# State-space stage of a decoder kernel: step sizes projected straight into token layout, and another order around it

## What is computed

```
zxbcdt = X @ W_in.T
z, xBC, dt = split(zxbcdt)                 # dt: 16 heads
dt  = softplus(dt + dt_bias)               # step sizes, token x head
xBC = silu(causal_conv4(xBC) + conv_b);  x, B, C = split(xBC)
dA  = exp(dt * -exp(A_log))
h_t = h_(t-1) * dA_t + dt_t * B_t x_t      # state recurrence, per head
y   = (C_t h_t + D * x) * silu(z);  y = rmsnorm(y) * norm_w
out = y @ W_out.T
```

## Time and profile before

| | |
|---|---|
| time, median of 3 runs | 1925.21 us (1923.62 to 1928.34) |
| profiled execution: time, span | 1927.49 us, 1925.8 us |
| busy share: TensorE, VectorE, ScalarE, GpSimd | 95%, 74%, 65%, 24% |
| mean granted clock of TensorE | 0.981 of full |
| state-space stage | about 0 to 810 us; a turn of its loop takes 97.06 us (line 581 starts at 386.26, 483.32 and 580.36) |

### The profile page before, as it was taken

How to read it: one execution, slowest core, us unless ns; L and a number is a source line. 1 busy time by engine, 2 the same in 40 slices (tenths; PEclk the granted TensorE clock), 3 DMA queues, 4 the chain that set the end, 5 groups by cost and what they waited for, 6 DMA issues and landing times. The chain is left out here.

```text
span 1925.8 us, 38879 instructions
## 1 busy us (share of the span) xinstructions
PE 1821.9 (95%) x12684; PEld 1299.9 (68%) x12684; DVE 1433.7 (74%) x2902; ACT 1257.5 (65%) x3128; POOL 469.1 (24%) x661
## 2 busy tenths in 40 slices
PE   7899999999999999778999999999999998799988
PEld 5677777777777778555666666666666664588853
DVE  8988888888888888646686867677777766655348
ACT  5646464646454555348888888888989887356514
POOL 1312121212121212331323232322323233100006
PEclk9999999999999999888999999999999999999999
DMA  7123131313131312333333333434343423811266
GB/s 236 53 55 97 49 103 49 103 47 105 46 105 44 107 45 88 135 100 97 88 111 111 111 111 101 121 90 123 89 121 91 124 70 122 280 48 59 73 205 254
DMA packets 121580, 200.60 MB, mean 104 GB/s; under 512 B 23856, under 2 KB 46384, under 8 KB 121136
## 3 DMA queue, kind: packets, MB, share of 16 engines
q1 hardware_dynamic: 112176, 179.21, 30.3%
q0 software_dynamic: 9216, 18.89, 3.9%
HBM read 117.27 MB, written 29.88 MB: 76 GB/s over the span
## 5 line engine op out<-in xcount | busy, mean ns | idle before, releaser
L2026 DVE TENSOR_REDUCE a_mx<-a_shared 128x1 f32<-128x512 f32 x512 | 329.1, 682 | 51.1 <-PE a_shared L2156 49.7
L1963 ACT ACTIVATE a_shared<-a_shared,a_mx 128x512 f32<-128x512 f32 x512 | 341.0, 668 | 23.4 <-DVE a_mx L2026 23.1
L1956 ACT ACTIVATE a_probs<-a_scores 128x512 f32<-128x512 f32 x512 | 300.7, 600 | 69.7 <-PE a_scores L2173 65.6
L2156 PE MATMUL a_shared<-a_ks,a_qs 96*128 96x512 f32 x512 | 208.9, 428 | 15.2 <-ACT a_shared L1963 10.9
L2173 PE MATMUL a_scores<-a_qs,a_ks 98*128 98x512 f32 x512 | 201.7, 405 | 6.1 <-ACT a_probs L1956 5.9
L2128 PE MATMUL a_shared<-link 128*128 128x512 f32 x768 | 199.4, 396 | 1.1 <-DVE a_qk_lo L2013 1.1
L1083 PE MATMUL m_proj<-m_xt_hi,link 128*128 128x512 f32 x448 | 182.0, 406 | 4.1 <-DVE m_acc L777 3.5
L2156 PEld LDWEIGHTS a_shared<-a_ks,a_qs 96*128 96x128 f32 x512 | 94.3, 190 | 130.7 <-ACT a_shared L1963 59.5
L597 ACT ACTIVATE m_xw<-m_added,m_wdt 128x64 f32<-128x64 f32 x256 | 56.0, 330 | 192.9 <-DVE m_xdt L865 192.8
L1084 PE MATMUL m_proj<-m_xt_lo,link 128*128 128x512 f32 x448 | 176.5, 394 | 0.0
L1085 PE MATMUL m_proj<-m_xt_hi,link 128*128 128x512 f32 x448 | 176.0, 393 | 0.0
(11 more groups left out here) (306 smaller groups left out, 3892.6 us busy)
## 6 DMA issues: line engine op xcount, KB each, us to landing
m_dec<-step_decay SPq DMA_DIRECT2D x64, 256.0 KB, 4.1
a_qs<-link SPq DMA_DIRECT2D x256, 64.0 KB, 2.1
m_ce<-run_decay SPq DMA_DIRECT2D x128, 112.0 KB, 3.0
a_ks<-a_k_hi POOLq DMA_DIRECT2D x192, 64.0 KB, 2.5
e_x<-x SPq DMA_DIRECT2D x11, 1024.0 KB, 5.6
m_xt_in<-x_t_in SPq DMA_DIRECT2D x8, 1024.0 KB, 9.5
m_x_tok<-x_in SPq DMA_DIRECT2D x8, 1024.0 KB, 5.4
x<-m_x_tok SPq DMA_DIRECT2D x32, 256.0 KB, 2.8
```

The costliest lines, as they stand in the source:

```text
L1956: act.activation(probs[:, n % 2, h, :], scores[t.score_bank(n, h)][:, :], ACT.Exp, scale=-1.0).then_inc(exp_ready, 1)
L1963: act.activation(scored[:, :], scored[:, :], ACT.Exp, scale=-1.0, bias=mx[:, i % 2, h, j:j + 1], accum_out=den[:, i, j, h:h + 1]).then_inc ...
L2026: dve.tensor_reduce(mx[:, i % 2, h, j:j + 1], bank(what)[:, :], AX.X, ALU.min).then_inc(mx_ready, 1)
L2156: pe.matmul(bank(what)[:, :], qs[0:STACK, t.slot(i), h, j * P:(j + 1) * P], ks[0:STACK, t.slot(i), h, :], start=True, stop=True).then_inc( ...
```

## The change

`dt_proj` keeps its place but swaps its operands: the 128-token slices of x are stationary and `w_dt` moves, so that the result is in token layout at once (32 matmuls of 32 columns instead of 8 of 512). ScalarE's copy and TensorE's turning matmuls go, and with them `dt_ch` and `pair_sum`; VectorE adds the high and low parts with one more instruction. On VectorE `raw_sizes` comes ahead of `states`, and `softplus` ahead of the B/C convolution. On ScalarE `step_exponents` comes ahead of the B/C tile's first tap. On TensorE x tile 0 comes ahead of `carried_outputs`. `tile_done` counts 17 for a sequence instead of 18, and `DT_STEPS` is 13 instead of 12.

```diff
--- before.py
+++ after.py
@@ -140,7 +140,6 @@
         win_hi, win_lo = (link[:, n * KT * COLS:(n + 1) * KT * COLS].rearrange("p (k c) -> p k c", k=KT)
                           for n in range(2))
         w_dt = sb("w_dt", [P, KT, 2 * NH], F32R)
-        pair_sum = sb("pair_sum", [2 * NH, NH])
         def over(name, tiles):
             return nc.alloc_sbuf_tensor_at("m_" + name, [P, tiles, SEQ], F32R, offset=-(-nc.sbuf_base // 32) * 32)
 
@@ -168,7 +167,6 @@
         xt_hi = sb("xt_hi", [P, KT, SEQ], F32R)
         xt_lo = sb("xt_lo", [P, KT, SEQ], F32R)
         x_tok = sb("x_tok", [P, TT, DM])
-        dt_ch = xt_in[0:2 * NH, 0, :]
         dt = sb("dt", [P, CH, NH])
         a = sb("a", [P, NH, CH])
         decay_t = sb("decay_t", [NH * CH, P])
@@ -216,7 +214,7 @@
         outp = [ps("outp0"), ps("outp1")]
         added = ctx.enter_context(nc.psum_tensor("m_added", [P, 2 * 512], F32))
         misc, turn = added[:, 0:512], added[:, 512:1024]
-        steps = proj[0]
+        steps = proj[0][:, 0:TT * 2 * NH].rearrange("p (c w h) -> p c w h", c=TT, w=2)
         mean = turn[:, 3 * CH * NH + P:3 * CH * NH + P + TT]
         xk_bank = [turn, outp[0]]
         yp = [ps("y0"), ps("y1")]
@@ -239,8 +237,7 @@
         x_in = sem("x_in")
         x_dbl = sem("x_dbl")
         tile_done = sem("tile_done")
-        dt_read = sem("dt_read")
-        dt_turned = sem("dt_turned")
+        dt_done = sem("dt_done")
         a_ready = sem("a_ready")
         sums_done = sem("sums_done")
         wd_ready = sem("wd_ready")
@@ -314,8 +311,9 @@
         next_stage = [(3, 1.0), (1, 1.0), (0, -SOFT_SCALE), (2, 1.0)]
 
         block = ctx.enter_context(nc.Block())
-        SET = 9
-        DT_STEPS = 12
+        SET = 8
+        DT_STEPS = 13
+        TILES = 1 + 2 * XT_TILES
         EARLY = 5
         DEC_CHUNK = 3
         CAST_FROM = 5
@@ -331,7 +329,6 @@
                 if not first:
 
                     sp.wait_ge(xt_split, at(b, KT, 0))
-                    sp.wait_ge(dt_turned, at(b, 1, 0))
                 sp.dma_start(xt_in[:, :, :], one(xT, b).rearrange("a (k p) n -> p (a k) n", p=P)
                              ).then_inc(xt_landed, 16)
 
@@ -419,7 +416,7 @@
                 for gr in range(2, NG):
                     load_carried(b, first, gr)
                 if not more:
-                    sp.wait_ge(tile_done, 18 * n_seq)
+                    sp.wait_ge(tile_done, TILES * n_seq)
                     for n, source in enumerate((one(ctxT, 0).rearrange("a (k p) n -> p (a k) n", p=P),
                                                 *(wT[w].rearrange("(k p) n -> p k n", p=P) for w in (1, 0, 2)))):
                         if n == 1:
@@ -469,8 +466,6 @@
             for r in range(2):
                 ins = pool.memset(parity[r * Q:(r + 1) * Q, r, :], 1.0)
             ins.then_inc(const, 1)
-            pool.tensor_tensor(pair_sum[:, :], ident[0:2 * NH, 0:NH], ident[0:2 * NH, NH:2 * NH], ALU.add
-                               ).then_inc(const, 1)
             pool.wait_ge(const, SET)
             def sum_squares(b, first, gr):
                 for j in range(2):
@@ -532,7 +527,7 @@
         def _(act):
             def conv_tap0(b, n, tile, slot):
 
-                act.wait_ge(tile_done, at(b, 18, tile + 1))
+                act.wait_ge(tile_done, at(b, TILES, tile))
                 act.activation(acc[:, slot, :], proj[tile % 2][:, :], ACT.Identity, bias=cb[:, n:n + 1],
                                scale=cw[:, n, 3:4]).then_inc(taps0, 1)
 
@@ -540,7 +535,7 @@
 
                 if not first:
 
-                    act.wait_ge(tile_done, at(b, 18, 0))
+                    act.wait_ge(tile_done, at(b, TILES, 0))
                 act.wait_ge(xt_landed, at(b, 16, 16))
                 for k in range(KT):
                     act.activation(xt_hi[:, k, :], xt_in[:, k, :], ACT.Copy).then_inc(xt_hi_s, 1)
@@ -571,14 +566,8 @@
 
             def z_silus(b, gr):
                 for j in range(2):
-                    act.wait_ge(tile_done, at(b, 18, 2 + 4 * gr + 2 + j + 1))
+                    act.wait_ge(tile_done, at(b, TILES, 2 + 4 * gr + 2 + j))
                     act.activation(zs[:, gr % 2, j, :], z_bank(gr, j)[:, :], ACT.Silu).then_inc(z_ready, 1)
-
-            def raw_steps(b, first):
-                act.wait_ge(tile_done, at(b, 18, 1))
-                if not first:
-                    act.wait_ge(dt_turned, at(b, 1, 0))
-                act.activation(dt_ch, proj[0][0:2 * NH, :], ACT.Copy).then_inc(dt_read, 1)
 
             def bc_tap0(b, first):
                 if not first:
@@ -609,8 +598,6 @@
             def gate_highs(b, part, more):
                 if part == 0 and more:
                     act.wait_ge(xt_split, at(b, KT, 2 * KT))
-                elif part == 1 and more:
-                    act.wait_ge(dt_turned, at(b, 1, 2))
                 for k in SPLIT_GATES[part]:
                     ins = act.activation(gate_high(k, more), g[:, k, :], ACT.Copy)
                 ins.then_inc(sq_ready, 1)
@@ -634,9 +621,9 @@
                 ins.then_inc(wd_ready, 1)
 
             def step_exponents(b):
-                act.wait_ge(dtv, at(b, DT_STEPS, 3))
+                act.wait_ge(dtv, at(b, DT_STEPS, 4))
                 act.activation(sm[:, 2], sm[:, 1], ACT.Exp).then_inc(dta, 1)
-                act.wait_ge(dtv, at(b, DT_STEPS, 4))
+                act.wait_ge(dtv, at(b, DT_STEPS, 5))
                 act.activation(sm[:, 4], sm[:, 3], ACT.Ln).then_inc(dta, 1)
 
             def bc_silus(b, first):
@@ -653,7 +640,6 @@
                 x_high(b, True)
                 act.wait_ge(small_in, 16 * N_SMALL)
                 act.activation(aneg[:, :], aneg[:, :], ACT.Exp).then_inc(dta, 1)
-                raw_steps(b, True)
                 bc_tap0(b, True)
                 step_exponents(b)
                 x_tap0(b, True, 0)
@@ -682,7 +668,6 @@
                 act.activation(wout_hi[:, :, :], wout_part, ACT.Copy).then_inc(const, 1)
 
             def next_head(done, b):
-                step_exponents(b)
                 x_tap0(b, False, 0)
                 bc_silus(b, False)
                 for j in range(2):
@@ -699,8 +684,6 @@
                         x_high(b + 1, False)
                     weighted_x(b, first, gr)
                     if gr + 1 == NG:
-                        if more:
-                            raw_steps(b + 1, False)
                         act.wait_ge(g_ready, gated_at(b, SPLIT_GATES[0][-1]))
                         gate_highs(b, 0, more)
                     if gr + 1 < NG:
@@ -713,6 +696,7 @@
                     if gr + 1 < NG:
                         silus(b, first, gr + 1)
                     elif more:
+                        step_exponents(b + 1)
                         bc_tap0(b + 1, False)
                     if first and gr == 0:
                         cast_columns(7)
@@ -792,16 +776,17 @@
             def raw_sizes(b, first):
 
                 dt_chain.start(b)
-                dve.wait_ge(dt_turned, at(b, 1, 1))
-                dt_chain.link(dve.tensor_tensor(sc[0].rearrange("p (c h) -> p c h", h=NH),
-                                                steps[:, 0:CH * NH].rearrange("p (c h) -> p c h", h=NH),
-                                                dtb[:, :].unsqueeze(1).to_broadcast([P, CH, NH]), ALU.add))
+                dve.wait_ge(dt_done, at(b, 1, 1))
+                raw = sc[0].rearrange("p (c h) -> p c h", h=NH)
+                dt_chain.link(dve.tensor_tensor(raw, steps[:, :, 0], dtb[:, :].unsqueeze(1).to_broadcast([P, CH, NH]),
+                                                ALU.add))
+                dt_chain.link(dve.tensor_tensor(raw, steps[:, :, 1], raw, ALU.add))
                 dt_chain.link(dve.tensor_scalar(sc[5], sc[0], -1.0, None, ALU.mult))
                 dve.tensor_tensor(sc[1], sc[0], sc[5], ALU.min).then_inc(dtv, 1)
 
             def softplus(b):
 
-                dt_chain.start(b, 3)
+                dt_chain.start(b, 4)
                 dve.wait_ge(dta, at(b, 2, 2))
                 dt_chain.link(dve.tensor_scalar(sc[3], sc[2], 1.0, None, ALU.add))
                 dt_chain.link(dve.tensor_scalar(sc[7], sc[3], 1.0, None, ALU.is_equal))
@@ -811,8 +796,8 @@
 
             def step_sizes(b, first):
 
-                dt_chain.start(b, 7)
-                dve.wait_ge(dtv, at(b, DT_STEPS, 7))
+                dt_chain.start(b, 8)
+                dve.wait_ge(dtv, at(b, DT_STEPS, 8))
                 dve.wait_ge(dta, at(b, 2, 3))
                 dt_chain.link(dve.tensor_tensor(sc[4], sc[4], sc[6], ALU.mult))
                 dt_chain.link(dve.tensor_tensor(sc[5], sc[4], sc[7], ALU.add))
@@ -830,7 +815,7 @@
                 dve.wait_ge(wd_ready, at(b, 2, 1))
                 if not first:
                     dve.wait_ge(decay_out, at(b, 32, 0))
-                dt_chain.start(b, 11)
+                dt_chain.start(b, 12)
                 for r in range(2):
                     half = slice(r * Q, (r + 1) * Q)
```

(32 more changed lines are left out.)

## The result

The kernel after takes 1970.86 us (median of 4 runs, 1965.92 to 1971.84), the kernel before 1924.41 (4 runs, 1921.74 to 1928.34): a ratio of 1.0228, with a 95% interval of 1.020 to 1.0256. So it is slower, as forecast, but by 46 us where the forecast had 18, and outside its range.

What follows compares the result with a forecast made beforehand. The prediction took TensorE's queue to set the pace. Head 3.9, first boundary 4.9, six boundaries at 0.71 and clock falls 5 summed to +18 us, put on the median as 1943 us, range 1929 to 1958.

Steps and rivals of the forecast that it cites:

- One record for each small matmul: Step projection on TensorE: each of 32 matmuls issued once, 0.11 us, 3.55 us together; the two-pass rival had chance 0.08.
- The gap of 81 ns: Step projection: the skill's spacing for load and matmul pairs, by which it would take 2.6 us; not used.
- The waits for `m_xw`: TensorE at the state matmuls: a 0.5 us wait that lies inside the new projection and goes.
- at the second z tile: TensorE later in the turn: a 0.54 us wait that goes, since VectorE has 1.18 us less to do there.
- x tile 0 does not wait for the step sums: TensorE at the boundary: VectorE's reads of the sums fit its idle time of about 1 us, costing nothing.
- The wait at x tile 1: TensorE waits 1.62 us for the B/C convolution, late behind softplus and step exponents; the no-wait rival had chance 0.07.
- A boundary without the clock: Between two sequences: -0.37 + 1.62 - 0.54 = +0.71 us, bounds -0.9 and +4.3.
- The head: Before the loop: the first projection at half clock, 6.7 us instead of 3.4, moving VectorE by +3.9 us.
- the first boundary: First change of sequence: projection and states at half clock, 9.7 us against 5.9; with the waits +4.9 us.
- the clock's term: Other six boundaries: half-clock falls of 0.5 to 2.7 us, 1.6 taken at three, +5; the unchanged-clock rival had chance 0.20.
- B: Start of the B/C tile on TensorE at a boundary, forecast at 485.8, 0.37 us earlier than before.
- the six boundaries +4.3: The boundaries after the first, without the clock: 6 x 0.71 us in the sum.

Runs made afterwards that it cites:

- experiment 6: Kernel after, loop start moved by 64 instructions, with three unused wide matmuls for every eight small ones of the projection: 1960.37 us, ratio 1.0184 to the kernel before.
- experiment 3: Kernel after plus 40 empty instructions ahead of the head, new projection kept but all engines' orders put back as before: 1951.69 us, ratio 1.0142.
- experiment 4: Kernel after plus 40 empty instructions, softplus put back behind the B/C convolution and step exponents behind its first tap: 1952.2 us, ratio 1.0145.
- experiment 5: Kernel before with softplus, step exponents and first x tile moved as in the change, old projection and turning step kept: 1932.7 us, ratio 1.0046.
- experiment 7: Kernel after plus 40 empty instructions, B/C tile's 12 wide matmuls among the small ones, its convolution ahead of states, both x tiles ahead of carried outputs: 1950.55 us.
- e1: Kernel after with 80 already satisfied waits (40 instructions) on TensorE ahead of the head, moving the loop's start: 1949.45 us, ratio 1.0123 to the kernel before.
- e3: The run of experiment 4: kernel after plus 40 empty instructions, softplus and step exponents in their old places: 1952.2 us, ratio 1.0145.
- e4: The run of experiment 3: kernel after plus 40 empty instructions, new projection with every old order: 1951.69 us, ratio 1.0142.
- e5: The run of experiment 7: kernel after plus 40 empty instructions, B/C tile's matmuls among the small ones, B/C convolution and x tiles moved earlier: 1950.55 us, ratio 1.0134.
- e6: The run of experiment 6: kernel after, loop start 64 instructions further on, 12 unused wide matmuls at each projection: 1960.37 us, ratio 1.0184.

## Why the prediction was too low

Right, point by point. One record for each small matmul, 0.11 us at full clock and 0.21 at half: 3.48 us from the first to the start of the last, so 3.6 for all where 3.55 was forecast, and 6.6 in the head where 6.7 was. The gap of 81 ns that the Trainium skill gives ("TensorE: Matmul & The Clock Gate", Back-to-back issue gap) is not that of this type and shape; the row of L1226 was the better guide. The waits for `m_xw` and at the second z tile are gone, and x tile 0 does not wait for the step sums. The wait at x tile 1 was forecast as 1.62 us and is 1.4 where the clock stays full (experiment 6); in the kernel after it is 1.0 at most, since falls ahead of it hide it in part. A boundary without the clock was forecast as +0.71; by experiment 6 it is 20.70 - 16.81 = 3.89, less the added 6.24 - 3.48 = 2.76, so +1.13 up to the decay sums, and -0.74 behind them: +0.39. The head (+3.9 forecast, +4.65 measured) and the first boundary (+4.9 forecast, 5.3 - 0.74 = +4.6 measured) were sized well.

Mis-sized, the clock's term: "what comes ahead of B doubles. That is 0.5 to 2.7 us, and I take 1.6 at three of the six: +5". The clock falls at six of six, and costs (19.6 - 6 x 1.13) / 6 = 2.1 us each, +12.8. The forecast took its falls as a matter of chance, from rows in which 128-column work with pauses was at the half level; the traces show that the new projection brings a fall at each boundary, with TensorE busy throughout (experiments 3 and 4, with little or no wait at x tile 1; and in the kernel after every fall begins 1.3 to 4.4 us behind the projection's start, ahead of that wait), that this wait and the new orders bring none (experiments 5 and 6), and that wide matmuls in between mostly prevent it (experiments 6 and 7). Why such matmuls lower the clock no run shows.

Left out, and the largest: no term for the jump of the loop. The sum went through the boundary's engines and never asked what else the 64 more instructions on TensorE do. They move the loop's start to a place where only two transposes get done behind the jump before TensorE stops: +18.9 us, about as much as the whole forecast. With head +3.9, first boundary +4.9, the six boundaries +4.3 and the clock +5 the forecast has 18; measured are 4.65, 4.6, 2.3 and 12.8, and 18.9 for the jumps: 43. Without the jumps the change would have been at e1's 1949 us, inside the range of 1929 to 1958, but with a clock term two and a half times the forecast's: the total alone would have hidden that.

That moving the start moves, shortens and removes the stop is shown (five positions, counted from the kernel before: 0 no stop, 48 1.9 us, 64 2.8 us, or 2.6 in the kernel after, 104 in e1, e3, e4 and e5 none, 128 in e6 none). That the stop is a wait for instructions on their way is argued, from "issue" and from the 1.2 to 1.5 us between the packet's end and the next matmul in all fifteen stops; no run here changed the transfer itself. Open too are why the falls last longer at some boundaries than at others, and where exactly the good and bad places for a loop's start lie.

## What to carry over

Count the instructions that a change adds ahead of a loop, and look at the first work behind each jump back: a wait put down to "issue" in the middle of a group of equal instructions is such a stop, and a few dozen empty instructions tell it apart from the change for the price of one run. They can also make one: 40 took the stops out of the kernel after, 48 put them into the kernel before. Split a slowdown by its place in the turn before splitting it by cause: no view of the boundary shows the largest part of this one. Where few wide matmuls give way to many narrow ones, put the clock into the sum at every occurrence: here it fell at six boundaries of six, though at full clock the state matmuls behind them start only 0.7 us later than before (3.7 us from the projection's start against 3.0).

## What was not expected of the hardware

- At a loop's jump back TensorE stopped for 1.7 to 3.0 us or not at all, by where the body starts; work went on 2.6 to 3.5 us after the body's first matmul, and 1.2 to 1.5 us after a packet of instructions had ended.
- 32 matmuls of 128 columns in the load and 32 in the stream took TensorE's granted clock from 1.00 to 0.50 within or behind their 3.5 us at six of six boundaries, though the engine was never idle; 12 unused wide matmuls among them kept it at 1.00 at five of six (e6), and the B/C tile's own twelve at six of six (e5).
- A wait ahead of x tile 1, of 1.2 us at the six boundaries of experiment 5 and of 1.4 us at the five of experiment 6 that kept their clock, did not lower it.
